# First window attention of a decoder kernel: scores from fp16 pairs on two halves of the TensorE array, the maximum as bias of the exponential, the rotary sines on GpSimd

## The reference

```
Q, K, V = (x @ Wq), (x @ Wk), (x @ Wv)            # 16 heads of 64, 8 batches of 256 tokens
Q = Q * cos + rotate_half(Q) * sin                 # rotary positions, the same for K
K = K * cos + rotate_half(K) * sin
scores = einsum('bhqd,bhkd->bhqk', Q, K) / sqrt(64)
scores = where(|q - k| <= 64, scores, -inf)        # a band of +-64 tokens
out = softmax(scores) @ V                          # then @ Wo, residual, layernorm
```

## Time and profile before

| | us |
|---|---|
| median of 3 runs | 1576.41 (1574.38 to 1583.6) |
| span of the profiled execution, first to last instruction | 1578.5 |
| PE / DVE / ACT / POOL busy in the span | 1208.8 / 1158.3 / 655.8 / 502.7 |
| window attention, from the start to its last instruction | about 0 to 549 |

### The profile page before, as it was taken

How to read it: one execution, slowest core, us unless ns; L and a number is a source line. 1 busy time by engine, 2 the same in 40 slices (tenths; PEclk the granted TensorE clock), 3 DMA queues, 4 the chain that set the end, 5 groups by cost and what they waited for, 6 DMA issues and landing times. The chain is left out here.

```text
span 1578.5 us, 29867 instructions
## 1 busy us (share of the span) xinstructions
PE 1208.8 (77%) x10299; PEld 990.4 (63%) x10300; DVE 1158.3 (73%) x2346; ACT 655.8 (42%) x1346; POOL 502.7 (32%) x494
## 2 busy tenths in 40 slices
PE   4889889888898789985016566588778946999687
PEld 1577676766777667774015566577667735777576
DVE  5687876777777558885945766469998984888678
ACT  3454543544444246553003332234343423555274
POOL 3212112121120035553552322135432323555222
PEclk7899999998999989995557887889988978999699
DMA  5000000100000000003322331120000002000001
GB/s 183 8 1 9 8 1 9 52 7 3 1 1 1 10 20 19 17 7 148 150 107 79 132 110 46 43 83 21 13 13 14 1 1 76 19 24 9 27 28 53
DMA packets 31080, 61.39 MB, mean 39 GB/s; under 512 B 7611, under 2 KB 20603, under 8 KB 27899
## 3 DMA queue, kind: packets, MB, share of 16 engines
q1 hardware_dynamic: 29434, 55.76, 10.0%
q0 software_dynamic: 1536, 4.20, 0.8%
HBM read 41.13 MB, written 10.42 MB: 33 GB/s over the span
## 5 line engine op out<-in xcount | busy, mean ns | idle before, releaser
L345 POOL TENSOR_TENSOR wa_rot<-wa_raw,wa_cos_sin 128x1024 f32<-128x1024 f32 x32 | 80.5, 2517 | 350.4 <-ACT wa_raw L389 348.0
L887 POOL TENSOR_TENSOR ca_z<-ca_z,ca_top 128x308 f32<-128x308 f32 x128 | 92.5, 722 | 133.9 <-DVE ca_top L1016 133.6
L639 PE MATMUL wa_scores<-wa_kt,wa_qt 128*128 128x192 f32 x512 | 121.5, 350 | 0.0
L2213 PE MATMUL re_g<-re_conv,re_w_g 128*128 128x256 f32 x512 | 112.8, 379 | 0.0
L2213 PEld LDWEIGHTS re_g<-re_conv,re_w_g 128*128 128x128 f32 x512 | 97.3, 190 | 13.2
L1143 PE MATMUL ca_turned<-ident,ca_probs 128*77 128x128 f32 x512 | 84.9, 289 | 21.0 <-ACT ca_probs L951 20.0
L959 ACT ACTIVATE ca_pth<-ca_turned 77x512 f16<-77x512 f32 x128 | 75.8, 592 | 60.3 <-PE ca_turned L1143 59.7
L1134 PE MATMUL ca_scores<-ca_km,ca_q 128*128 128x308 f32 x256 | 90.1, 435 | 5.9 <-ACT ca_q L932 5.6
L605 PE MATMUL wa_shared<-wa_wh,wa_xh 128*128 128x512 f16 x192 | 76.7, 399 | 19.8 <-ACT wa_raw L389 10.1
L1021 DVE SCALAR_TENSOR_TENSOR ca_ptl<-ca_turned,ca_pth 77x512 f16<-77x512 f32 x128 | 86.7, 677 | 2.9 <-ACT ca_pth L959 2.9
L639 PEld LDWEIGHTS wa_scores<-wa_kt,wa_qt 128*128 128x128 f32 x512 | 80.2, 197 | 13.3 <-issue 1.2
(11 more groups left out here) (310 smaller groups left out, 3924.5 us busy)
## 6 DMA issues: line engine op xcount, KB each, us to landing
ex_stage<-in_ew SPq DMA_DIRECT2D x16, 1024.0 KB, 6.8
ca_xs<-tokens SPq DMA_DIRECT2D x16, 256.0 KB, 2.4
slots<-rt_zeros SPq DMA_DIRECT2D x4, 920.0 KB
wa_w_stage<-in_wqkv SPq DMA_DIRECT2D x6, 512.0 KB, 4.5
ex_xe<-slots SPq DMA_DIRECT2D x16, 160.0 KB, 2.3
slots<-ex_y SPq DMA_DIRECT2D x15, 160.0 KB
wa_x_stage<-in_xt SPq DMA_DIRECT2D x8, 256.0 KB, 3.3
tokens<-in_x SPq DMA_DIRECT2D x1, 2048.0 KB, 10.6
```

Source lines behind the costliest of these rows:

```text
L345: pool.tensor_tensor(rot[:, r % 2], raw[:, r % 2], c, ALU.mult).then_inc(cos_done, 1)
L639: ins = pe.matmul(dst, qt[par][:, 2 * u + h, t * P:(t + 1) * P], kt[par][:, u, t * WINDOW:t * WINDOW + SPAN], start=False, stop=True)
L887: pool.tensor_tensor(z[k][:], z[k][:], top[:, k].unsqueeze(2).broadcast_to((P, UH, CTX)), ALU.subtract).then_inc(shift, 1)
L2213: ins = pe.matmul(g_bank[m][:, k], w_g[:, j, cols], conv[par][:, j], start=(j == 0), stop=(j == HT - 1))
```

## The change

It does four things, all inside the window attention:

- Q and K after rotation are kept as a pair of fp16 values (high `qh`, `kh` and low `ql`, `kl`) in place of one float32. ScalarE writes the high part of each turn (one full-width copy), VectorE the low part (`turned_low`, new), and only VectorE's instruction frees the bank.
- A score is the sum of three fp16 products (high x high, high x low, low x high) with a contraction of 64 rows: head 0 of the pair on rows 0 to 63 of the array, head 1 on rows 64 to 127, issued in turn. The mask is one product of 384 columns per head. A score bank now holds one head and both tiles, and PE waits for the exponentials (`exped`) before it overwrites one.
- The maximum is no longer subtracted by VectorE. A product of 2 columns makes `minus_top`, and ScalarE takes it as the bias of the exponential, straight out of PSUM, in four instructions of 192 columns per unit. In ScalarE's order the exponentials of unit u+1 now stand in slot u behind its first step.
- The two sine products of a rotation go from VectorE to GpSimd, behind the cosine product. The layer norm moves from slot 4 to slot 5 on VectorE. The zeroing of `qt` on GpSimd at the start goes.

The core of the diff:

```diff
+QSCALE = 16.0
+SSCALE = HD ** -0.5 / (QSCALE * QSCALE)
@@ gpsimd
-            def cosine(b, r):
+            def rotate(b, r):
...
                 pool.tensor_tensor(rot[:, r % 2], raw[:, r % 2], c, ALU.mult).then_inc(cos_done, 1)
+                for a, z in ((0, HD // 2), (HD // 2, 0)):
+                    s = cos_sin[:, r // 2, 1, a:a + HD // 2].unsqueeze(1).broadcast_to((P, HEADS, HD // 2))
+                    ins = pool.tensor_tensor(sine[:, r % 2, :, a:a + HD // 2], raw[:, r % 2, :, z:z + HD // 2], s, ALU.mult)
+                ins.then_inc(sin_done, 1)
@@ scalar, a turn
-                        act.activation(qt[par][0:HD, 8 * c:8 * c + 8:2, cols], s[0:HD], ACT.Copy)
-                        act.activation(qt[par][HD:P, 8 * c + 1:8 * c + 8:2, cols], s[HD:P],
-                                       ACT.Copy).then_inc(free[bank], 1)
+                    high = qh if c < 2 else kh
+                    act.activation(high[par][:, 4 * (c % 2):4 * (c % 2) + 4, cols], s, ACT.Copy,
+                                   scale=QSCALE).then_inc(qk_high, 1)
@@ scalar, new
+            def exponentials(b, u):
+                for h in range(2):
+                    n = 2 * u + h
+                    k = 2 * (u % 2) + h
+                    act.wait_ge(shift, b * 16 + n + 1)
+                    if not (first(b) and u < 2):
+                        act.wait_ge(probs_t, b * 16 + n - 3)
+                    for t in range(TPB):
+                        ins = act.activation(probs[k][:, t, t * WINDOW:t * WINDOW + SPAN], s_bank[h][:, t, 0:SPAN], ACT.Exp,
+                                             scale=SSCALE, bias=minus_top[:, k, t:t + 1])
+                    ins.then_inc(exped, 1)
@@ scalar, in a slot
+                    steps = WA.slot(slot, b)
+                    for n, (kind, i, bank, uses) in enumerate(steps):
                         d = WA.serves(kind, i)
                         step(b + d, (par + d) % 2, kind, i, bank, uses)
+                        if n == 0:
+                            next_exponentials(b, slot, after)
+                    if not steps:
+                        next_exponentials(b, slot, after)
@@ vector, new; sin_part goes
+            def turned_low(b, par, i, bank):
...
+                dve.wait_ge(qk_high, b * 8 + i + 1)
+                dve.scalar_tensor_tensor(out=low[par][:, pairs, cols], in0=shared[bank][:].rearrange("p (h q) -> p h q", h=4),
+                                         scalar=QSCALE, in1=high[par][:, pairs, cols], op0=ALU.mult,
+                                         op1=ALU.subtract).then_inc(free[bank], 1)
@@ vector, take_maximum in place of shift_scores
                     dve.wait_ge(scores, b * 16 + n + 1)
+                    dve.tensor_reduce(top[:, k], s_bank[h][:, :, 0:SPAN], AX.X, ALU.max).then_inc(maxed, 1)
+                    dve.wait_ge(maxed, b * 16 + n + 1)
                     if not (first(b) and u < 2):
                         dve.wait_ge(exped, b * 16 + n - 3)
-                    dve.tensor_tensor(shifted[k][:], s_bank[t][:, :, 0:SPAN],
-                                      top[:, k].unsqueeze(2).broadcast_to((P, 2, SPAN)), ALU.subtract).then_inc(shift, 1)
+                    dve.tensor_scalar(minus_top[:, k], top[:, k], -SSCALE, None, ALU.mult).then_inc(shift, 1)
@@ tensor, score
+                for h in range(2):
+                    if not (first(b) and u == 0):
+                        pe.wait_ge(exped, b * 16 + 2 * u + h - 1)
+                    pe.matmul(s_bank[h][:, :, 0:SPAN], ident_bf[:], band[:], start=True, stop=False)
                 for t in range(TPB):
+                    tok, keys = slice(t * P, (t + 1) * P), slice(t * WINDOW, t * WINDOW + SPAN)
+                    for n, (q, k) in enumerate(((qh, kh), (qh, kl), (ql, kh))):
+                        for h in range(2):
+                            rows = slice(h * HD, (h + 1) * HD)
+                            ins = pe.matmul(s_bank[h][:, t, 0:SPAN], q[par][rows, u, tok], k[par][rows, u, keys],
+                                            start=False, stop=(t == TPB - 1 and n == 2))
+                            if t == TPB - 1 and n == 2:
+                                ins.then_inc(scores, 1)
```

More of the change, by code:

```diff
@@ L355, in _ @@
             for r in range(4):
-                cosine(0, r)
+                rotate(0, r)
             batch(0, before=False)
@@ L430, in batch, with next_exponentials @@
                         act.activation(windows(pth[k][:]), windows(t_bank[h][:]), ACT.Copy, scale=PSCALE).then_inc(probs_high, 1)
+            def next_exponentials(b, slot, after):
+                if slot < 7:
+                    exponentials(b, slot + 1)
+                elif after:
+                    exponentials(b + 1, 0)
             split_x(0, 0)
@@ L435, in _ @@
             for kind, i, bank, uses in WA.prologue():
-                if (kind, i) == ("turn", 0):
-                    act.wait_ge(zeroed, 1)
-                    act.wait_ge(qt_zeroed, 4)
                 step(0, 0, kind, i, bank, uses)
+            act.wait_ge(zeroed, 1)
+            exponentials(0, 0)
             batch(0, 0, before=False)
@@ L459, in split_x @@
                                          in1=xh[:, par], op0=ALU.mult, op1=ALU.subtract).then_inc(x_low, 1)
-            def sin_part(b, r):
-                wait_raw(dve, b, r)
-                if not (first(b) and r == 0):
-                    dve.wait_ge(rope_done, b * 4 + r)
-                for a, z in ((0, HD // 2), (HD // 2, 0)):
-                    s = cos_sin[:, r // 2, 1, a:a + HD // 2].unsqueeze(1).broadcast_to((P, HEADS, HD // 2))
-                    ins = dve.tensor_tensor(sine[:, :, a:a + HD // 2], raw[:, r % 2, :, z:z + HD // 2], s, ALU.mult)
-                ins.then_inc(sin_done, 1)
             def add_part(b, r):
@@ L539, in batch @@
                             value_low(b + 1, 1 - par, i, bank)
+                        if kind == "turn":
+                            turned_low(b + 1, 1 - par, i, bank)
                         if kind == "mix":
@@ L543, in batch @@
                         add_part(b + 1, ROPE_ADD[slot])
-                    if after and slot in ROPE_SIN:
-                        sin_part(b + 1, ROPE_SIN[slot])
-                    if before and slot == 4:
+                    if before and slot == 5:
                         layer_norm(b - 1, 0)
@@ L572, in _ @@
                     r = 2 * (i // 6) + (i % 6) // 2
-                    sin_part(0, r)
                     add_part(0, r)
-            shift_scores(0, 0, 0)
+                if kind == "turn":
+                    turned_low(0, 0, i, bank)
+            take_maximum(0, 0)
             dve.wait_ge(tokens_loaded, 16)
```

69 lines of the change are left out of this document (25 added, 44 removed).

## The result

The changed kernel takes 1614.64 us (median of 4 runs, 1613.54 to 1617.04); the kernel before, on the same chip, 1575.39 (1574.03 to 1583.6). The ratio is 1.0228, interval 1.019 to 1.0267. The prediction was 1573, with a range from 1546 to 1600. It is wrong: the change is slower, by more than the range allowed. The medians are 39 us apart, the spans of the two profiled executions 33.3; the kernel before was profiled in an execution some 5 us above that median (its span plus the 1.7 us by which time and span differ in the other runs). What follows accounts for the 33.3.

The account below looks back on a forecast made before the run. PE nearly back to back, VectorE close behind. Slots -3.95 and clock +2.5 gave -1.45 a batch, -10 over seven; batch 7 +3.5, prologue +3.3: about -3, median 1573, own range 1562 to 1590, with rivals 1546 to 1600.

Parts of the forecast that it names:

- the clock term: Batches with projections: slow clock charged 1.5 us for slot 2's new stall and 1.0 for slots 6, 7, 0: +2.5.
- the ring: Slots 6, 7 and 0, and batch 7: VectorE and ScalarE wait on each other without overlap, 4.05 us a slot.
- slot 5's 8.8: Slot 5 forecast at 8.8 us, before 11.63, including a PE stall of 3.0 and a heads 1 wait of 0.75.
- the price of `minus_top`: VectorE: 16 small products a batch, each priced 0.154 us like a product of one column, +2.4 a batch.
- PE loses 7.5 us of work a batch: Support for faster: PE loses 7.5 us and VectorE 7 a batch; slack in the chains goes to PE at once.
- Scores: Score call on PE: masks 0.33 plus six fp16 pairs 0.48, in all 0.80 us instead of 1.74, gain 0.94 a unit.
- that rival: Scores: the two halves do not overlap, +0.48 in slots 1, 3 and 4, seven times: 1583; chance 0.10.
- ScalarE: Exponentials of 192 columns: 0.33 us each, four about 1.1 where two were about 0.94; ScalarE's sum level, its order not.
- Slots 6, 7 and 0: VectorE leaves slot 5 about 2.3 us behind PE; slots forecast 3.4 + 4.5 + 7.5, 15.4 us, before 15.78.
- The prologue: Before the first score: additions wait for 4.6 us of GpSimd instead of 2.4, last turns 2 us later: +3.3.
- The clock falls further: Rival: some 30 us of a batch run at clock 0.78 instead of 0.93, +3.7 a batch, 1599; chance 0.18.
- The chains are shorter: Rival: shorter chains and the clock stays, 1556, or 1545 also without holds by GpSimd; chance 0.30.

Follow-up runs that it names:

- e9_fill: Changed kernel with unread products on PE in its two stalls, 12 before turn 1 in slot 2, 14 before turn 4 in slot 5: 1596.80 us, ratio 1.0100.
- e10_before_fill: Kernel before the change, with 20 unread products on PE before turn 4 in slot 5: 1579.49 us, ratio 0.9995.
- e5_negmax: Changed kernel without the `minus_top` instruction; the maximum is written negated and is itself the bias: 1596.08 us, ratio 1.0089.
- e4_late_exp: Changed kernel with the exponentials of unit u+1 behind all steps of slot u in ScalarE's order: 1583.42 us, ratio 1.0015.
- e6_late_negmax: Changed kernel with exponentials behind all steps of the slot and the maximum written negated, no `minus_top` instruction: 1568.64 us, ratio 0.9922.
- e7_sines_alone: Kernel before the change, with only the sine products moved to GpSimd, using one sine buffer: 1580.65 us, ratio 1.0003.
- e1: Changed kernel with the two sine products back on VectorE: 1637.44 us, ratio 1.0358.
- e8_late_slot2: Changed kernel with the exponentials behind all steps in slot 2 only, behind the first step elsewhere: 1594.17 us, ratio 1.0078.

## Why the prediction was wrong, step by step

The forecast was -10 for the seven batches with projections, +3.5 for batch 7, +3.3 for the prologue and 0 behind: -3. Measured were +23.1, +2.6 (with the tail), +4.1 and +3.5: +33.3. Of the miss of 36, the seven batches are 33 and the untouched stages 3.5; prologue and tail all but cancel. Of the 33, slot 5 makes about 12, batch 0 about 8, slots 1 to 4 about 7, slots 6, 7 and 0 about 4, the loop's head 2.5. For batches 1 to 6, means of the changed kernel against my slots:

```
               predicted    measured    what the difference is
slot 1            6.3         6.53      entering and leaving the half mode
slot 2       7.7 + 1.5        9.41      right in the mean
slot 3           13.4        13.91      the same as slot 1, and late heads
slot 4            6.3         6.52      as slot 1
slot 5            8.8        10.73      clock behind the stall 1.35, sizes 0.5
slots 6, 7, 0   15.4 + 1.0   17.3       project 0 waits 1.7 for x's low part
loop's head   as before   6.3, 6.6      second gap (4.7 and 5.7 before)
```

**The first failed step is the clock term, "I charge the new stall of slot 2 the same and the ring 1.0".** I had read from the earlier trace rows that 1.5 us are lost behind a stall of 4.16. Then I charged that to the new stall and forgot the one that stayed: slot 5's 8.8 has a stall of 3.0 and full speed behind it. The stall measured 2.85, and behind it the clock was 0.65; `e9_fill` puts the price at 1.2 to 1.6 a batch, 10 us in seven, and `e10_before_fill` gives the same 1.4 a batch for the stall of 4.15. The term was not too uncertain, it was left out. The stall of the old kernel got shorter by 1.3 us and kept its whole clock price. It is the largest single term of the miss, and not all of it.

**The second is the price of `minus_top`, 0.154 from the earlier trace rows with no hold.** I had allowed additions and sines of VectorE to be held by GpSimd, since both had rows that showed it, and took a product of one column, which had run in no such place, as free of it. It meets a rotation in slot 1. In the stretch from 60 to 500 us:

```profile
L517 DVE TENSOR_SCALAR wa_minus_top<-wa_top 128x2 f32<-128x2 f32 x106 | 32.8, 309 | 6.2 <-DVE wa_top L513 1.5
```

That is a mean of 309 ns instead of 154, and single ones of 2.18 and 2.29 us, while the maximum next to it (0.55) is at most 0.56. `e5_negmax` gives the price of the whole instruction: 17 us. The sum had 0.15 us for each; how much of the miss the holds are is open, and as fewer holds also mean shorter stalls and a better clock, this price and the 10 us above overlap and can't be added. The Trainium skill (SBUF — State Buffer, Who interferes with whom) says that a `tensor_scalar` can take the port pair that VectorE shares with GpSimd, that whoever comes second is blocked for the whole instruction, and that a `tensor_reduce` on trn2 never contends. This case's trace doesn't show the ports; it agrees with the blocking (the ends of the two products above), with the reduction at 0.55 beside it, and with GpSimd's side too: in the batch at 200 us a sine pair there takes 3.47 us instead of 2.49.

**The third is what I did with the order.** The stalls themselves were named and sized rightly: slot 2 2.7 (2.36 in four batches, 3.4 in two), slot 5 3.0 (2.85), heads 0 0.94 (0.92), heads 1 0.75 (0.77), batch 7 4.05 a slot (4.07 in two of them). The chains were right, so the mechanism was on paper. I took "PE loses 7.5 us of work a batch" as the income and the new stalls as a small cost, and never priced the alternative order, in which the exponentials stand behind the copies. `e4_late_exp` shows what stood there to be found: 30 us for the place of one call. This explains the loss, not the miss: the stalls were in the sum. What failed with them is the balance, in which income of 7.5 us a batch was to outweigh them.

**Scores.** The sum of 0.80 was short of the overheads. From the first mask (284.06) to the first product it is 0.42, 0.09 over two masks of 384 columns; six pairs take 0.50; the next step starts at 285.08, 0.09 after the last pair's share. The call takes 1.02. The halves do overlap, so that rival is out. The Trainium skill (TensorEngine Tiling, Key Properties) has a change of tiling mode drain the array; the rows fit that, with about 0.09 at each change, 0.2 a call, where I had worked out 0.3. It shows as the 0.2 in slots 1, 3 and 4, some 4 to 5 us in all.

**ScalarE.** An exponential of 192 columns from PSUM takes 0.42, not 0.33, and four of them 1.35 to 1.42, not 1.1. Each is in the chain of slots 2 and 5 and is part of slot 5's 0.5.

**Slots 6, 7 and 0.** The ring between VectorE and ScalarE is there in batch 7, where slots 1, 2 and 0 take 4.08, 4.07 and 4.00; slot 4 takes 2.71 there and slot 5 4.81, so that it is partly luck that its +2.6 comes near the forecast of +3.5. In the other batches slot 6 takes 4.9, slot 7 3.5 and slot 0 8.8, against 3.4, 4.5 and 7.5. Missing in my sum is project 0, which waits 1.7 us for the low part of the next batch's x: VectorE makes that in slot 0 and comes to it late.

**The prologue** was right in kind and 0.8 short: the wait for `value_low` went from 5.62 to 8.00 us. Batch 0 cost 6.2 more than before and I had given it no steps of its own; 5.0 of that is heads 0, the long wait in the fourth row of PE's waits, with a clock of 0.50 behind it (slot 3 of batch 0 takes 12.81 instead of 6.48).

**The rivals.** "The clock falls further" was the nearest, with 0.18 and 1599, and its mechanism is not what happened. I had the mean clock at 0.9 and was right (0.91 to the start of the cross attention), and the rival asked for 0.78 everywhere. What mattered is where the slow stretches lie: behind the stalls PE is the bound. "The chains are shorter" (0.30) is the reverse of what was measured; only `e6_late_negmax` comes near to it. The chance of 0.22 for slower was too small for a change that adds waits for the same slot's results to an in-order queue.

## What to carry to other kernels

When an in-order engine takes over a result of the same slot, price its place in the order against the next one before you price the work it saves; here the place was worth 30 us, and without that loss the whole change came out level with the kernel before (`e4_late_exp`, 1.0015). Behind PE's stalls of 2.85 and 4.15 us the slow clock cost about 1.4 us more in this kernel; each remaining stall of such a length gets a term like that in a forecast, old ones too. A tiny VectorE instruction between a maximum and its reader was not free here beside a busy GpSimd; let the reduction give the value with its sign.

## What the runs showed of the hardware

**Which stalls bring the clock down.** For every stall of PE from 100 to 500 us I read the granted clock of the 3 us behind it. In the changed kernel, `e5_negmax` and `e6_late_negmax`, all stalls of 1.1 to 1.3 us have 1.00 behind them, and of the twelve of 1.6 to 1.8 all but one (0.61). In `e9_fill` one of 1.58 has 0.70 behind it and one of 1.74 has 0.59. Between 1.9 and 2.9 us the same stall is followed by 0.5 to 1.00 from batch to batch: 2.36 by 1.00, 0.67, 0.59 in slot 2 of the changed kernel, 1.94 by values from 0.57 to 1.00 in `e4_late_exp`. From 3.1 up, all but one have 0.50 to 0.81 behind them; the one is a gap of 3.39 at the loop's head of `e7_sines_alone` (371 us), with 1.00. So equal stalls differ, and no length that always or never does it is claimed.

**The loop's head.** At the jump back PE has a gap of 2.9 to 3.8 us that no engine ends ("issue"), in all kernels. In most there is a second of 2.1 to 3.2 us right behind it, with a clock of 0.50 after it: in the changed kernel, `e1` to `e6`, `e8_late_slot2` and `e10_before_fill`, not in the kernel before, `e7_sines_alone` or `e9_fill`. The trace of `e9_fill` lacks it and that of `e10_before_fill` has it, the reverse of their base kernels, and the products of neither stand near the jump. At each of two jumps it costs 2.4 us in `e10_before_fill`. What decides it was not tested, and with one trace of each kernel it is open whether the kernel or the execution does.
